# Post-norm attention and expert layer: the final layer norm moved into the expert blocks, and the attention part's transfers split and reordered

## The reference

```python
q = softmax(x @ Wq, axis=-1); k = softmax(x @ Wk, axis=-2); v = x @ Wv
ctx = einsum('bnd,bne->bde', k, v) / sqrt(16)
x = layernorm(x + (einsum('bnd,bde->bne', q, ctx) / 256) @ Wo + bo)
vals, idx = top_k(x @ wr.T, 2)        # two experts for each token
gate = softmax of the two vals        # an expert takes at most 5120 tokens
h = gelu(xg @ w1[e] + b1[e]); y = h @ w2[e] + b2[e]
out = sum of gate * y over the token's experts
x = layernorm(x + out)
```

## Time and profile before

| | us |
|---|---|
| median of 3 runs | 2362.0 (2361.18 to 2364.57) |
| profiled execution | 2358.53, its span 2356.6 |
| attention part, entry of the expert part included | 0 to 741.5 |
| expert blocks | 741.5 to 2247.8 |
| after the last matmul | 2247.8 to 2356.6 |
| PE busy | 2049.0 (87%) |
| DVE, ACT, POOL busy | 1113.5, 1136.2, 1111.8 (47, 48, 47%) |
| moved | 190.10 MB, mean 81 GB/s |

### The profile page before, as it was taken

One profiled execution on the slowest core, in us unless ns is written; L12 is line 12 of the kernel. 1 busy time (PEld: TensorE's weight loads), 2 busy tenths in 40 slices (PEclk: granted clock), 3 DMA queues, 4 the chain that ended last, 5 costly groups with the idle time before them and its releaser, 6 DMA issues. The chain is left out here.

```text
span 2356.6 us, 48196 instructions
## 1 busy us (share of the span) xinstructions
PE 2049.0 (87%) x16208; PEld 1987.8 (84%) x16209; DVE 1113.5 (47%) x2614; ACT 1136.2 (48%) x2516; POOL 1111.8 (47%) x1333
## 2 busy tenths in 40 slices
PE   7887887878744999999999999999999999999910
PEld 6776786777644999999999999999999999999910
DVE  3665565655563435345335333534543534333345
ACT  3444443434332555555555455455455555555547
POOL 0335454453544445444455444544544545444434
PEclk9998898989876999999999999999999999999965
DMA  4323233242223323222322322322322222222258
GB/s 165 108 73 124 90 103 111 72 143 71 68 81 95 80 46 81 45 45 45 79 47 49 76 45 47 80 45 45 80 45 45 45 45 46 46 46 46 46 204 377
DMA packets 130733, 190.10 MB, mean 81 GB/s; under 512 B 19088, under 2 KB 111760, under 8 KB 126480
## 3 DMA queue, kind: packets, MB, share of 16 engines
q0 software_dynamic: 58256, 68.60, 18.1%
q1 hardware_dynamic: 72448, 121.16, 14.8%
HBM read 104.05 MB, written 85.66 MB: 81 GB/s over the span
## 5 line engine op out<-in xcount | busy, mean ns | idle before, releaser
L1031 ACT ACTIVATE h_ps<-h_ps,b_sb 128x256 f32<-128x256 f32 x1032 | 418.5, 444 | 712.6 <-PE h_ps L1129 667.7
L988 POOL DMA_INDIRECT sum_rows<-y,put_idx x260 | 418.9, 1611 | 601.6 <-DVE y L1055 556.3
L1066 DVE TENSOR_TENSOR h_lo<-h_ps,h_hi 128x512 fp32r<-128x512 f32 x516 | 356.6, 691 | 628.7 <-ACT h_hi L1034 600.5
L1145 PE MATMUL y_ps<-w_hi,h_hi 128*128 128x256 f32 x2064 | 586.1, 284 | 0.0
L1129 PE MATMUL h_ps<-bt_hi,w_hi 128*128 128x256 f32 x2064 | 576.1, 279 | 3.2 <-issue 1.7
L1145 PE MATMUL y_ps<-w_hi,h_lo 128*128 128x256 f32 x2064 | 575.8, 279 | 0.0
L1145 PE MATMUL y_ps<-w_lo,h_hi 128*128 128x256 f32 x2064 | 575.1, 279 | 0.0
L1129 PE MATMUL h_ps<-bt_lo,w_hi 128*128 128x256 f32 x2064 | 574.0, 278 | 0.0
L1129 PE MATMUL h_ps<-bt_hi,w_lo 128*128 128x256 f32 x2064 | 574.0, 278 | 0.0
L323 POOL DMA_INDIRECT slot_table<-entry,where x256 | 277.8, 1085 | 304.2 <-DVE entry L575 228.7
L1129 PEld LDWEIGHTS h_ps<-bt_hi,w_hi 128*128 128x128 f32 x2064 | 389.6, 189 | 5.0 <-issue 3.2
(11 more groups left out here) (191 smaller groups left out, 2843.9 us busy)
## 6 DMA issues: line engine op xcount, KB each, us to landing
xt_raw<-in_x_t SPq DMA_DIRECT2D x16, 1024.0 KB
x_raw<-in_x SPq DMA_DIRECT2D x16, 1024.0 KB
w_raw<-in_w SPq DMA_DIRECT2D x16, 1024.0 KB
x_rows<-x_sb SPq DMA_DIRECT2D x16, 1024.0 KB
sum_rows<-x_sb SPq DMA_DIRECT2D x16, 1024.0 KB
s_in<-sum_rows SPq DMA_DIRECT2D x16, 1024.0 KB, 8.9
out<-s_out SPq DMA_DIRECT2D x16, 1024.0 KB, 6.8
rows<-x_rows,pick_idx POOLq DMA_INDIRECT x260
```

The costliest lines, as they stand in the source:

```text
L988: pool.indirect_dma_start(out=acc_dram, out_offset=bass.IndirectOffsetOnAxis(ap=put_idx[:, t:t + 1], axis=0), in_=y[:, t, :], in_offset=No ...
L1031: nc.scalar.activation(half, half, ACT.Gelu_apprx_tanh, bias=b1_sb[:, bass.ds(e * FT + 2 * g + i, 1)]).then_inc(gelu_done, 1)
L1066: V.tensor_tensor(h_lo[:, g, :], h_ps[:, g, :], h_hi[:, g, :].bitcast(F), ALU.subtract).then_inc(h_lo_done, 1)
L1145: ins = nc.tensor.matmul(y_ps[:, t, :], v[:, g, h:h + P], w[:, c:c + D], start=(f == 0 and t == 0 and part == 0), stop=(f == FT - 1 and t ...
```

## The change

It does the following.

1. The third part is gone. The expert part finishes rows itself. A token's first expert (the lower slot number, a "lead") starts from the token's own x1 row, the second from the row that the first has written to `out`; the second one normalizes the sum, the first stores it as it is. An entry has 4 words for this: token, token or an out-of-range number for leads (then nothing is gathered), gate, and the flag of the last.
2. In a block, ACT copies the gathered rows to `x1_next` (`keep_rows`) and to `base` (`lay_base`); POOL gathers `out` rows over `base` (`take_up_sums`), takes the root (`root`), and puts by a plain write. DVE adds (`add_up`), makes statistics (`spread`), factors and rows (`factors`, `finish_rows`), and copies the index columns and gates (`base_of`, `pick`, `gates`), which POOL did before. The first block of an expert puts before it takes up; the second adds late.
3. In the attention part ACT also writes to `out` the row of a token with no expert, layer norm of x1 (`renormalize`, tile `alone`; POOL `norm_again` makes its factor), 2 x 512 KB a batch; the copy to `sum_rows` is gone. DVE's router has five more small operations a batch.
4. SP's transfers of the attention part are halves and quarters, each behind its own event.
5. PE does `up(3)` ahead of `down(0)`. The weights are split in blocks 0, 2 and 3 of an expert. Every expert does at least 5 blocks instead of 4 (all have more here).

The core of the diff:

```diff
-                def body(pair, u, x_left=True, xt_left=True):
+                def body(pair, u, x_left=True, xt_left=True, second=False):
                     b = pair * 2 + u
                     if x_left:
-                        sp.wait_ge(r_done, (b + 1) * TILES)
-                        load_x(b + 2, u)
+                        sp.wait_ge(r_done, b * TILES)
+                        for j in range(PAIRS):
+                            sp.wait_ge(kt_used, PAIRS * b + j + 1)
+                            load_x(b + 1, 1 - u, j)
+                    if not second:
+                        for half in range(2):
+                            store_alone(b - 2, half)
+                    store_x1(b - 1, 1 - u, 0)
                     if xt_left:
-                        sp.wait_ge(xt_lo_done, b + 4)
-                        load_xt(b + 4)
-                    sp.wait_ge(x1_done, b + 1)
-                    for rows in (x1_store, acc_store):
-                        sp.dma_start(rows[b].rearrange("p (t d) -> p t d", d=D), x1_sb[u][:, :, 0:D]).then_inc(x1_stored[u], 16)
+                        sp.wait_ge(xt_lo_done, b + 3)
+                        load_xt(b + 3, 0)
+                        sp.wait_ge(r_done, b * TILES + 4)
+                        load_xt(b + 3, 1)
+                    store_x1(b - 1, 1 - u, 1)
...
+                def norm_again(b, u):
...
+                    nc.gpsimd.tensor_tensor(again[u][:, :], mean_var[:, :, 1], rstd[:, :], ALU.mult).then_inc(again_step, 1)
...
+                    nc.gpsimd.tensor_tensor(again[u][:, :], again[u][:, :], minus_half[:, :], ALU.pow).then_inc(again_done, 1)
...
+                def renormalize(b, u):
+                    act.wait_ge(again_done, b + 1)
...
+                            ins = nc.scalar.activation(alone[:, t, :], x1_sb[u][:, t, 0:D], ACT.Copy, scale=again[u][:, t:t + 1])
+                        ins.then_inc(alone_done, 1)
...
+                        V.tensor_tensor(leads[:, 0, :], slot_i[:, 1, :], slot_i[:, 0, :], ALU.is_ge)
+                        step(V.tensor_tensor(leads[:, 1, :], slot_i[:, 0, :], slot_i[:, 1, :], ALU.is_ge))
...
+                def first_body(n, e, eu):
+
+                    gather(n + 1)
+                    root(n)
+                    put(n)
+                    pool.wait_ge(put_done, 16 * BT * (n + 1) + 16)
+                    take_up_sums(n)
 
                 def body(n, e, eu):
-                    pool.wait_ge(xt_ready, n + 1)
                     gather(n + 1)
+                    root(n)
+                    take_up_sums(n)
                     put(n)
...
+                def lay_base(n):
+
+                    act.wait_ge(sum_step, STEPS * n + 1)
+                    act.wait_ge(next_done, n + 1)
+                    nc.scalar.activation(base[:, :, :], x1_next[:, :, :], ACT.Copy).then_inc(base_done, 1)
...
+                def spread(n):
+                    dve.wait_ge(sum_step, STEPS * n + 1)
+                    for t in range(BT):
+                        ins = V.bn_stats(stats[:, t, :], y_raw[:, t, :])
...
+                    late = turn == 1
+                    if not late:
+                        add_up(n)
+                        base_of(n)
+                        spread(n)
                     for g in range(UNITS):
                         dve.wait_ge(h_hi_done, n * UNITS + g + 1)
                         V.tensor_tensor(h_lo[:, g, :], h_ps[:, g, :], h_hi[:, g, :].bitcast(F), ALU.subtract).then_inc(h_lo_done, 1)
-                        if g == 1:
-                            scale_y(n)
+                        if late and g == 1:
+                            add_up(n)
+                            base_of(n)
+                            spread(n)
+                        if g == (2 if late else 0):
+                            factors(n)
+                            finish_rows(n)
                         if g == UNITS - 1:
                             split_lo(n + 1)
...
                     up(2)
+                    up(3)
                     down(0)
-                    up(3)
                     transpose_rows(n + 1)
```

More of the change, by code:

```diff
@@ L123, in build @@
             rstd, nshift = sb("rstd", [P, TILES]), sb("nshift", [P, TILES])
+            again = [sb(f"again{i}", [P, TILES]) for i in range(2)]
+            alone = sb("alone", [P, TILES, D])
             minus_half = sb("minus_half", [P, TILES])
@@ L426, in body @@
                         q_softmax(b + 1, 1 - u, 1)
+                    if not first and not (isinstance(b, int) and b == 1):
+                        renormalize(b - 2, u)
                     if not first:
@@ L942, in experts, with column @@
                         blocks, before = blocks_of(eng, half * 2 + eu)
-                        with eng.Fori(0, blocks) as block:
+                        if first_body is not None:
+                            first_body(before, half * 2 + eu, eu)
+                        with eng.Fori(0 if first_body is None else 1, blocks) as block:
                             body(before + block, half * 2 + eu, eu)
+            def column(n, w):
+                return table[:, bass.ds(n * BT, BT), w]
             @block_b.sync
@@ L1000, in _ @@
+                wait_apart(pool, pick_ready, 1)
+                for t in range(BT):
+                    pool.indirect_dma_start(
+                        out=rows[:, t, :], out_offset=None, in_=x1_dram,
+                        in_offset=bass.IndirectOffsetOnAxis(ap=pick_idx[:, t:t + 1], axis=0)).then_inc(gathered, 16)
                 for e in range(1, E):
[L1001 removed]
+                    before = pool.value_load(plan[0:1, E + e:E + e + 1], min_val=5 * e, max_val=e * BLOCKS)
@@ L1034, in body @@
                         nc.scalar.activation(h_hi[:, g, :], h_ps[:, g, :], ACT.Copy).then_inc(h_hi_done, 1)
+                        if g == late_base:
+                            lay_base(n)
                     split_hi(n + 1)
-                experts(act, body)
+                    keep_rows(n + 1)
+                with act.Fori(0, E // 2) as half:
+                    for eu in range(2):
+                        e = half * 2 + eu
+                        blocks, before = blocks_of(act, e)
+                        body(before, e, eu)
+                        body(before + 1, e, eu, 2)
+                        with act.Fori(2, blocks) as block:
+                            body(before + block, e, eu)
             @block_b.vector
@@ L1088, in expert @@
                     blocks, before = blocks_of(dve, e)
-                    for turn in range(2):
-                        body(before + turn, e, eu, None if last else turn)
-                    with dve.Fori(2, blocks) as block:
+                    for turn in range(4):
+                        body(before + turn, e, eu, turn, not last)
+                    with dve.Fori(4, blocks) as block:
                         body(before + block, e, eu)
```

356 lines of the change are left out of this document (201 added, 155 removed).

## The result

The changed kernel takes 2343.9 us (median of 13 runs, 2325.3 to 2353.3) against 2363.4 for the kernel before (13 runs, 2359.0 to 2368.2): a ratio of 0.9912, 95% interval 0.9892 to 0.9932. That is 19.5 us faster, where 186 were forecast, and outside the stated 2135 to 2250 us. The profiled execution took 2345.2 us, its span 2343.4.

What follows compares the result with a forecast made beforehand. It took attention to be bound by stops from instruction fetch behind SP's transfers, the experts by PE, the last pass by transfers. 2358.5 - 92 - 97 + 3 + 0 = 2172.5, plus 3.5 to the median: 2176 us, range 2135 to 2250.

Steps and rivals of the forecast that it cites:

- The separate pass: After the last matmul: the 108.8 us layer-norm pass goes, a 17 us tail replaces it; gain 92 us, bounds 89 to 95.
- The term for landing and block end: In the tail after the last matmul: 8.4 us of the 17 us, for the last put's landing and the block end.
- The attention part: Batches fall from 41.7 to 35.0 us as SP's transfers are spread; gain 97 us, bounds 58 and 132.
- What bounds the kernel now: Attention part: PE, DVE and ACT stop 8 to 9 us, read as instruction fetch through DMA engines saturated by SP's transfers.
- I leave 1 us of stall: Attention part: smaller SP clusters leave 1 us of stop a batch, added to POOL's 34.1 us loop for 35.0.
- mostly hidden: The skill's rule that instruction refills are mostly hidden; taken against the fetch reading, it would leave attention at 41.7 us a batch.
- the stall is not the transfers' doing: Rival, attention part: engines stop whatever SP does, so only the pass is gained, less 1 us a batch; 2286 us, chance 0.10.
- The other three rivals: Blocks: PE waits 0.9 us each, 2292 (0.09); SP's transfers in series, 2456 (0.02); POOL bounds the expert part, 2602 (0.02).
- POOL's loop as the next bound: Attention part: scatters, norm chain and new operations take POOL 34.1 us a batch, above PE's 32.3.
- Entry of the expert part: Start of the expert part: larger table rows land and copy later, delaying DVE's first gate; cost 3 us, bounds 0 and 8.
- The expert blocks: 129 blocks of 11.68 us: 5 us gained on gather waits, 5 lost on late h_lo; net 0, bounds -7 and +25.
- thinnest cover: Expert blocks: DVE's work reaches 11.5 us in blocks that split weights, just under the 11.68 us of a block.

Runs made afterwards that it cites:

- Runs 1 to 5: Attention part's 16 indirect transfers removed from changed kernel (31.48 us a batch) or kernel before (31.33); pows after pairs in changed (36.95) or before (36.34); pows ahead, changed (48.63).
- run 12: Changed kernel with pows breaking up indirect transfers in both parts, and each attention batch's 16 transfers in two rows of eight: 2195.6 us, ratio 0.9307, batch 31.93 us.
- run 3: Changed kernel with a small POOL pow after every second indirect transfer of the attention part: 2299.6 us, ratio 0.9662, batch 36.95 us.
- run 11: Changed kernel with a pow after every second indirect transfer in the attention part and two pows per expert block: ratio 0.9589 to the kernel before.
- Run 8: Changed kernel with two pows per expert block, between sums and puts and behind the puts, plus two added tiles: 2342.6 us, ratio 0.9827.

## Why the prediction was wrong, point by point

- **The separate pass** (gain 92, bounds 89 to 95): right in kind, measured 97.3, above its bounds. The term for landing and block end, 8.4 us, was mis-sized: the last put's issue ends at 2340.8 and the span at 2343.4, 2.6 us later, and the whole tail is 11.5 us.
- **The attention part** (gain 97): wrong, and the largest miss; it lost 5.4 us up to batch 15's first context matmul instead. The step that failed is the reading under "What bounds the kernel now": that the engines stop for instructions fetched through saturated DMA engines. It rested on two things that happened together, SP's cluster and the stop. POOL's transfers, the third thing in the same stretch, were dismissed with "POOL carries on", as if an engine that works could not be the cause. Runs 1 to 5 show that it was. With the cluster and without the row a batch takes 31.33 us; with the row whole and seven pows ahead of it, 48.63; with the row broken up by the same pows, 36.95 and no such stop. From the wrong cause came "I leave 1 us of stall", and 35.0 for 42.35. The remark that the stops begin where the loop begins was a coincidence as well: the first scatter is in batch 1's body, at 89 us.
- **The Trainium skill's "mostly hidden"** (Runtime: NRT & Kernel Launch, Instruction fetch mechanics), which spoke against my reading, was right for most of the loop: five back edges of PE's loop and no packet of instructions in 350 us. At two changes of expert three packets stand beside stops of DVE's of 5.07 and 5.64 us, and run 12 has both stops again (5.2 us each). That the fetch makes them was read from the trace and not tried in a run.
- **The rival "the stall is not the transfers' doing"**, 0.10, had the attention part right: batches of 42.4, where it had 42.7. Its 2286 is still 58 us too low, since it took the blocks at net 0. The other three rivals did not come: PE waited for h_lo 30 us in all and not 116, SP's parts did not hold up a batch, and no indirect transfer of the expert part averages over 1.05 us.
- **POOL's loop as the next bound** (34.1 us): right as a mechanism, hidden behind the hold in the changed kernel, where POOL still waits 14.5 us a batch for the entries. Once the hold is gone the loop decides: 36.9 us with seven pows in run 3, and the same in run 11. Run 12 puts more on POOL and takes 31.93 us a batch, since half of the row is off the way from the entries to the norm chain.
- **Entry of the expert part** (cost 3): the first y_raw stands 101.3 us after batch 15's first context matmul, before 98.0. Right.
- **The expert blocks** (net 0, bounds -7 and +25): 75.4 us longer, outside the bounds. The duration terms held: a gather 1.01 us, a plain put 1.02, the pow 0.72, and the short blocks at 11.47 us are even 0.1 shorter than before, which may be the reordering's gain and was not tried. What failed is "Six indirect transfers at 1.3 plus pow 1 is 8.8 ... under 11.68": their cost was taken as POOL's time alone. Four transfers in pairs make no y_raw late, six in a row up to 3.2 us at the block's end. Of the 75.4, 39 are the 30 long blocks less what the short ones gain, and 36 the first five blocks of each expert, some 11 of it at the two changes with fetched instructions. Run 8 takes the hold away, and its expert part is still 62.9 us longer than before; less the estimated 54 us of the two tiles, 9 are left. So by that estimate some 66 of the 75.4 us are the hold, and without it the part would have been within the bounds.
- **VectorE's "thinnest cover"**: 8.5 and 3.3 us are 11.8 and not 11.5, above the 11.68 of a block. Measured are 8.0 us a block on average (1033 us in 129 blocks), and PE waits 30 us in all for h_lo. The cover was thinner than said, and it was not what failed.

## What to carry to other kernels

When several engines stop together while their inputs exist, ask what the one engine that still works is doing; before putting a stop down to something that coincides with it, take that thing away once. Count indirect transfers on POOL by how closely they follow one another, not only by POOL's time: here two pairs a block were free, and six or sixteen in a row at 1.3 us were not, so let them go out in short groups, with POOL's other work between them and where nobody waits for PE. A wait called "remote" on a PE result whose matmul has long ended is the sign to look for. When such a stop is mended, look at the waits again before calling the rest a remainder of it: here the rest was POOL's loop. And an edit that declares a tile moves the tiles behind it; 16 bytes a partition cost 0.4 us a block here, so a control must declare them too.

## What was not expected of the hardware

- PE's semaphore updates come late while POOL issues indirect transfers closely. In the attention part before, updates with three starts in the 5.5 us ahead of their matmul's end came 0.12 us late on average, with four 1.7, with five 4.6; after, 0.07, 1.3 and 5.2; with two or fewer 0.01 in both. Matmuls without an update of their own (26 before, 55 after, all close to a transfer) are left out. By what path POOL reaches PE stays open.
- It does not depend on the rows moved (64 or 128 partitions, batches of 42.4 us in both), nor on a neighbour (0.2 us of other work between two changes nothing), and 0.72 us of other work after every second transfer takes the stops away.
- Updates of PE are missing from the record only near indirect transfers: from 89 to 600 us 50 of 200 in the changed kernel, 131 of 361 in run 12, none of the others. In run 12 at 247.69 a matmul has no update, and ACT's qt_hi, which waits for it, starts at 247.93. A missing record is thus no late update.
- Two tiles of 8 bytes a partition, declared ahead of the others, set PE's h_ps matmuls 120 ns apart instead of 114 in eight kernels, used or not.
- The blocks of the expert part lock into one of two rhythms, 11.47 or about 13 us, and stay in the long one for up to a dozen blocks; where POOL's row falls in the block differs between the two, and that this sets the rhythm is argued from the rows, not tried.
